# Group weights of the expert stage: one matmul per batch and row loads from DRAM in place of eight matmuls and eight evictions

## The chip, the cores and the metric

The kernel runs on one core of a Trainium2 chip. The metric is the device time of one execution in microseconds (us). Three runs of the kernel before gave a median of 1887.81 us (1886.92 to 1889.61).

## The reference

Two layers of gated attention and feed-forward are applied to `x`, 8 batches of 512 tokens by 512 features; each part adds `tanh(gate)` times its result to `x`. The change touches only the last part, the experts' layer:

```python
logits = jnp.einsum('th,eh->te', x, gate_weight)          # 32 experts
probs = jax.nn.softmax(logits)
top_val, top_idx = jax.lax.top_k(probs, 8)
top_val = top_val / jnp.sum(top_val, axis=-1, keepdims=True)
onehot = jax.nn.one_hot(merge_groups[top_idx], 8)
w_tg = jnp.einsum('tk,tkg->tg', top_val, onehot)          # weight of each of 8 groups
...                                                       # 8 groups of 192 hidden units
act = jax.nn.silu(gate) * up
y = jnp.einsum('tgi,ghi->tgh', act, dn)
out = jnp.einsum('tg,tgh->th', w_tg, y)
```

So each token has one weight for each of 8 groups, and that weight multiplies the 192 hidden units of the group before the down projection.

## The kernel before, in words

Everything is written out by hand from one list of steps, `make_plan()`. Each of the five engines walks through that same list in order and picks out the steps that concern it, so the list sets the order of work on every engine, on the queue of transfers (engine SP issues them all) and on PE. Semaphores join the engines.

The work has three stages: attention over 8 batches, the first feed-forward layer (until about 1063 us), and the expert stage with the second attention in between (from about 1063 us to the end). Weights and activations are kept as pairs of f16 tiles (high part, low part), so a projection of 128 output rows by 512 tokens takes 12 matmuls: three passes over four slices of 128.

**The expert stage** has 8 blocks, one for each batch b, of 12 steps j (8 groups of 192 rows are 1536 rows, 12 tiles of 128). One step, as (b, j), is:

- `ge` and `ue`: 12 matmuls each (line 923, in `project`), into one PSUM bank each. ScalarE (ACT) applies silu to the first (L1215), VectorE (DVE) multiplies the second by it (L1648), into one of three tiles `prod_s`.
- `mix`: DVE multiplies this tile by the group's weights (L1660) into `mact_s`; a tile that spans two groups (j = 1, 4, 7, 10) takes two instructions of 64 rows each. ACT rounds the result to f16 (L1228), GpSimd (POOL) makes the low part (L897).
- `dn` of the step before: 12 matmuls (L1092) that add into banks 0 to 3. `dn(b, j)` stands in the list behind `ge` and `ue` of step j+1, and waits for POOL's low part.

Before the first `mix` that uses group gg, the list has `bw(b, gg)`: PE multiplies `onehot` (a 0/1 matrix of 128 columns for each group, made once on DVE at L1410) by `wTs`, the turned weights of the 32 experts, so that all 128 output rows hold the weight of group gg (L1079); ACT evicts the bank into one of three tiles `gw_s` (L1223), and `mix` reads it. `bw(b, 0)` and `bw(b, 1)` come in steps 0 and 1, the others in steps 3, 4, 6, 7, 9 and 10.

Between these steps a list of side tasks of the next batch is taken one by one (`attention_tasks`): statistics (L1278, L852, L1283), norms (L1291) and turns on PE (L932, copied at L1131 and L1299), the attention over 64 context rows (`cxsplit`, L1522 and L1524, to `read`, L1587), the router, and `rturn` (L1063), which turns the experts' weights and leaves them in `wTs` (L1639). The two side tasks in step j = 1 and the one at the end of step 0 are: statistics of batch b+1 (step 0), then `cxsplit(b+1)` with `cxload(b+2)` and the first norm (step 1).

**The queue of engine SP** takes in block b, in the order of the list:

1. `xstore(E, b-1)`, 1 MB, L749, after the last `res3` of the block before (L1666, DVE, which follows the last `dn` of the batch);
2. `xload(E, b+2)`, 1 MB, L738, which waits until that store has landed;
3. `cxload(b+2)`, three transfers of 128 KB each, L809 to L811, which wait for `cxsplit(b+1)` on ACT and DVE in step 1.

The loads exist in blocks 1 to 5; blocks 6 and 7 have the store alone. Ahead of block 0 come the store of the stage before and `xload(E, 1)` and `xload(E, 2)` together (L738), which wait for that stage's last matmul; `cxload(2)` comes in its step 1.

```python
            elif kind == "mix":
                ...
                for gg in groups_of(j):
                    rows = slice(max(gg * INTER - j * P, 0), min((gg + 1) * INTER - j * P, P))
                    w.wait_ge(bw_ok, NG * b + gg + 1)
                    of = gw_s[(NG * b + gg) % 3]
                    e.tensor_tensor(r[rows, :], of[rows, :], m[rows, :], ALU.mult).then_inc(mixed)
```

Of the kernel before, what the change touches and what calls it, by code (L numbers as in the profile page):

```python
# [101 lines left out]
def make_plan():  # L102
# [260 lines left out]
    def attention_tasks(b):  # L363
        L, M = ln_tasks(("L", b)), ln_tasks(("M", b))

        def split():
            add("cxsplit", b)
            if b + 1 < NB:
                add("cxload", b + 1)

        def both(f, g):
            def go():
                f()
                g()
            return go
        return [L[0], both(split, L[1]), L[2], L[3], L[4], L[5], L[6],
                lambda: add("scores", b, banks=1), lambda: None, lambda: add("pturn", b, banks=1),
                lambda: add("read", b, banks=NT), *M, lambda: add("router", b, banks=1), lambda: None, lambda: None,
                lambda: add("rturn", b, banks=1)]

    for J in range(total + 2):
        if J < total:
# [31 lines left out]
    for J in range(total + 1):  # L414
        if J < total:
            b, j = divmod(J, NR)
            add("ge", b, j, banks=1)
            add("ue", b, j, banks=1)
            if side:
                side.pop(0)()  # L420
            for gg in range(j * P // INTER, ((j + 1) * P - 1) // INTER + 1):
                if gg * INTER >= j * P:
                    add("bw", b, gg, banks=1)
            add("mix", b, j)
        if J >= 1:
            bd, jd = divmod(J - 1, NR)
            add("dn", bd, jd)
            if jd == NR - 1:
                for t in range(NT):
                    add("res3", bd, t)  # L430
                if bd < NB - 1:
                    add("xstore", "E", bd)
                if bd + 3 < NB:
                    add("xload", "E", bd + 3)
        if J < total and j == 0 and b + 1 < NB:
            side = attention_tasks(b + 1)
        if side:
            side.pop(0)()
# [1 line left out]


def build(nc, x_in, ctx_in, ctx_t, mask_in, gx_in, gf_in, wq, wg, bg, wkv, wo, w1, b1, w2, b2,
          gw, gup, dnp, mg, dom, xa, xb, yscr, out, stack):
    plan = make_plan()
    nth, bank_of = plan.nth, plan.bank
    KB = 256
# [63 lines left out]
    prob = at(185, NT * NE).rearrange("p (t s) -> p t s", t=NT)  # L510
    prep = at(185.5, NT * NE).rearrange("p (t s) -> p t s", t=NT)
    wcat = small(NT * P // 2, F16).rearrange("p (t s) -> p t s", t=NT)
    onehot = small(NG * P // 2, F16)
    ctr = small(NC * CTX).rearrange("p (c s) -> p c s", c=NC)
    bgT, b1T = small(NC), small(NH)
    inv = {n: small(1) for n in ("q", "g", "1", "gate", "up", "gw")}
# [46 lines left out]
    def sem(name):  # L563
        return stack.enter_context(nc.semaphore(name))
# [27 lines left out]
    sc_mm, soft, sc_exp, p_turned, p_copied = (sem(n) for n in ("sc_mm", "soft", "sc_exp", "p_turned", "p_copied"))  # L592
    rd_mm, rd_c, rd_res = sem("rd_mm"), sem("rd_c"), sem("rd_res")
    r_mm, rout, r_exp, r_turned, r_copied = (sem(n) for n in ("r_mm", "rout", "r_exp", "r_turned", "r_copied"))
    ge_mm, silu, ue_mm, prod, bw_mm, bw_ok, mixed, m_hi, m_lo, dn_mm = (
        sem(n) for n in ("ge_mm", "silu", "ue_mm", "prod", "bw_mm", "bw_ok", "mixed", "m_hi", "m_lo", "dn_mm"))

    SOFT, ROUT = 13, 21
    C_MS, C_ID, C_ALL = 8, 9, 20
# [11 lines left out]
    def freed(step, i):  # L611
        kind, n = step[0], nth[step]
        if kind == "turn":
            return y_lo, n
        if kind == "q":
            return q_relu, n
        if kind == "gate":
            return g_tanh, n
        if kind == "kvk":
            return k_phi, n  # L620
        if kind == "kvv":
            return v_max, n
        if kind == "kvsum":
            return sum_ok, 4 * (n - 1) + i + 1
        if kind == "numden":
            return nd_mul, 2 * (n - 1) + i + 1
        if kind == "att":
            return a_gated, n
        if kind == "out":
            return res1, n  # L630
        if kind == "up":
            return gelu, n
        if kind == "scores":
            return soft, SOFT * (n - 1) + 4
        if kind == "pturn":
            return p_copied, n
        if kind == "read":
            return rd_res, NT * (n - 1) + i + 1
        if kind == "router":
            return rout, ROUT * (n - 1) + 1  # L640
        if kind == "rturn":
            return r_copied, n
        if kind == "ge":
            return silu, n
        if kind == "ue":
            return prod, n
        assert kind == "bw"
        return bw_ok, n


    x_slot = {("A", b): b % 3 for b in range(NB)}
# [58 lines left out]
    def bcast(v):  # L710
        return v.partition_broadcast(P)


    def sync_program(e):
        w = Once(e)
        regs = {}
        for step in plan.steps:
# [72 lines left out]
            elif kind == "small":  # L790
                e.dma_start(gains[:, 0:2], bcast(gx_in)).then_inc(small_in, 16)
                e.dma_start(gains[:, 2:4], bcast(gf_in)).then_inc(small_in, 16)
                e.dma_start(masku.bitcast(I32), bcast(mask_in.rearrange("b s -> (b s)"))).then_inc(small_in, 16)
                e.dma_start(bgT, bg.rearrange("(j p) -> p j", p=P), allow_slow_non_contiguous=True).then_inc(small_in, 16)
                e.dma_start(b1T, b1.rearrange("(j p) -> p j", p=P), allow_slow_non_contiguous=True).then_inc(small_in, 16)
                e.dma_start(mgi[0:NE, :], mg.rearrange("(e o) -> e o", o=1)).then_inc(small_in, 16)
                e.dma_start(mgi[NE:2 * NE, :], mg.rearrange("(e o) -> e o", o=1)).then_inc(small_in, 16)
                e.dma_start(domt[0:1, :], dom.rearrange("(o g) -> o g", o=1)).then_inc(small_in, 16)
            elif kind == "b2":
                w.wait_ge(a_turned, nth["att", NB - 1, NT - 1])  # L800
                e.dma_start(gb2, bcast(b2)).then_inc(b2_in, 16)
            elif kind == "cxload":
                b = step[1]
                if b == 0:
                    w.wait_ge(w_lo, nth["wlo", N_D - 1])
                else:
                    w.wait_ge(c_hi, 2 * b)
                    w.wait_ge(c_lo, 2 * b)
                e.dma_start(craw[0:CTX, :], ctx_in[b]).then_inc(craw_in, 16)  # L809
                e.dma_start(craw[CTX:P, :], ctx_in[b]).then_inc(craw_in, 16)  # L810
                e.dma_start(ctr, ctx_t[:, b * CTX:(b + 1) * CTX].rearrange("(c p) s -> p c s", p=P)).then_inc(craw_in, 16)  # L811
# [6 lines left out]
    def pool_program(e):  # L818
        w = Once(e)
        e.memset(ident, 0.0).then_inc(const)  # L820
        e.memset(bmask, 0.0).then_inc(const)
        e.memset(onehot, 0.0).then_inc(const)
        e.memset(wcat[:, :, :], 0.0).then_inc(const)
        e.memset(clo, 0.0).then_inc(const)
        e.memset(ones, 1.0).then_inc(const)
# [83 lines left out]
    def tensor_program(e):  # L909
# [25 lines left out]
        for step in plan.steps:  # L935
# [134 lines left out]
            elif kind == "ue":  # L1070
                _, b, j = step
                w.wait_ge(w_lo, n_lo["up"])
                project(step, upT, j, yT[b % 2], ue_mm)
            elif kind == "bw":
                _, b, gg = step
                k = bank_free(step)
                w.wait_ge(r_copied, b + 1)
                w.wait_ge(dconst, 13)
                e.matmul(bank[k][:, :], onehot[:, gg * P:(gg + 1) * P], wTs[b % 2], start=True, stop=True).then_inc(bw_mm)  # L1079
            elif kind == "dn":  # L1080
                _, b, j = step
                hv = macth_s[(n - 1) % 3]
# [40 lines left out]
    def scalar_program(e):  # L1123
        w = Once(e)
        for step in plan.steps:
# [81 lines left out]
            elif kind == "ge":  # L1207
# [5 lines left out]
                if n > 3:  # L1213
                    w.wait_ge(prod, n - 3)
                e.activation(silu_s[(n - 1) % 3], bank[bank_of[step, 0]][:, :], ACT.Silu,  # L1215
                             scale=inv["gate"]).then_inc(silu)
            elif kind == "bw":
                _, b, gg = step
                w.wait_ge(bw_mm, n)
                w.wait_ge(cd_ok, 1)  # L1220
                if n > 3:
                    w.wait_ge(mixed, mix_last(n - 3))
                e.activation(gw_s[(n - 1) % 3], bank[bank_of[step, 0]][:, :], ACT.Copy, scale=sc["kd"]).then_inc(bw_ok)  # L1223
            elif kind == "mix":
                w.wait_ge(mixed, mix_value(n))
                if n > 3:
                    w.wait_ge(dn_mm, dn_value(n - 3))
                e.activation(macth_s[(n - 1) % 3][0][:, 0, :], mact_s[(n - 1) % 3], ACT.Copy).then_inc(m_hi)  # L1228
# [18 lines left out]
    def vector_program(e):  # L1247
# [17 lines left out]
        for step in plan.steps:  # L1265
# [136 lines left out]
            elif kind == "tables":  # L1402
# [4 lines left out]
                w.wait_ge(dconst, 5)  # L1407
                w.wait_ge(const, C_ALL)
                for gg in range(NG):
                    e.tensor_scalar(onehot[0:2 * NE, gg * P:(gg + 1) * P], ones[0:2 * NE, :], mgf[0:2 * NE, :],  # L1410
                                    float(gg), ALU.mult, ALU.is_equal).then_inc(dconst)
            elif kind == "ctxmax":
                w.wait_ge(ctx_in_s, 16)
                e.tensor_reduce(sc["mc"], ctxT.rearrange("p t n -> p (t n)"), AX.X, ALU.max,
# [217 lines left out]
            elif kind == "rturn":  # L1632
# [2 lines left out]
                if b == 0:  # L1635
                    w.wait_ge(w_lo, nth["wlo", N_D - 1])
                if b > 1:
                    w.wait_ge(bw_mm, NG * (b - 1))
                e.tensor_copy(wTs[b % 2], bank[bank_of[step, 0]][:, :].bitcast(F16)[:, 0:TOK]).then_inc(r_copied)  # L1639
            elif kind == "ue":  # L1640
                _, b, j = step
# [8 lines left out]
            elif kind == "mix":  # L1650
# [4 lines left out]
                    w.wait_ge(m_lo, n - 3)  # L1655
                for gg in groups_of(j):
                    rows = slice(max(gg * INTER - j * P, 0), min((gg + 1) * INTER - j * P, P))
                    w.wait_ge(bw_ok, NG * b + gg + 1)
                    of = gw_s[(NG * b + gg) % 3]
                    e.tensor_tensor(r[rows, :], of[rows, :], m[rows, :], ALU.mult).then_inc(mixed)  # L1660
            elif kind == "res3":
                _, b, t = step
# [47 lines left out]
```

## Time and profile before

| what | value |
|---|---|
| median of 3 runs | 1887.81 us |
| the profiled execution's own time | 1887.19 us |
| its span in the trace | 1885.4 us |
| instructions | 24612 |
| moved by transfers | 112.10 MB, mean 59 GB/s |
| TensorE's mean granted clock | 0.993 of full speed |

The profiled execution is one run; its own time is 1.8 us more than the span of the trace, and 0.6 us less than the median of the three runs. Times in the trace count from the start of the span. A PE matmul of 512 columns is shown 379 ns long, but matmuls are pipelined: one starts some 0.216 us after another, so busy time adds up from starts, not from these lengths. "To landing" is the time from a transfer's issue until its semaphore is complete. The idle time in square brackets in a timeline is that of the engine just before the instruction, with the one that released it.

### The profile page before, as it was taken

The page shows a single profiled execution, that of the slowest core. Times are in us where ns is not written, and L with a number is a line of the kernel's source. Part 1 is how long each engine was busy: PE and PEld are TensorE (multiplying, and loading weights), DVE is VectorE, ACT ScalarE, POOL GpSimd, SP SyncE. Part 2 cuts the span into 40 slices and gives each one's busy share as a digit, 9 for nine tenths or more (in the row PEclk, how much of TensorE's full clock was granted, in tenths as well). Part 3 has the DMA queues.
Part 4 walks back from the last instruction along what each step waited for, and adds up shares of the span by engine and source line. Part 5 has one row for each costly group of instructions (what it writes and reads, how often), then busy time and mean ns, then how long its engine had stood idle before and what let it go on. Part 6 is the DMA issues. An engine that isn't in the chain of part 4 may idle for free.

```text
span 1885.4 us, 24612 instructions
## 1 busy us (share of the span) xinstructions
PE 1846.4 (98%) x9552; PEld 905.6 (48%) x9552; DVE 995.9 (53%) x2036; ACT 538.6 (29%) x801; POOL 323.5 (17%) x299
## 2 busy tenths in 40 slices
PE   8799999999999999999999999999999999999999
PEld 3445554644444444444444444444444444444444
DVE  5676776754554455454436554545445455554422
ACT  3224433312221122122112233233333223333321
POOL 1123322222021120202010011111111111111111
PEclk9899999999999999999999999999999999999999
DMA  5124433333414223340310200101010101000000
GB/s 159 55 62 129 140 118 95 96 129 65 104 42 127 90 68 104 70 125 27 90 54 9 76 1 23 32 1 54 1 54 1 54 1 54 1 23 1 1 23 23
DMA packets 135830, 112.10 MB, mean 59 GB/s; under 512 B 75554, under 2 KB 92066, under 8 KB 135714
## 3 DMA queue, kind: packets, MB, share of 16 engines
q1 hardware_dynamic: 135714, 110.53, 19.7%
q8 instruction: 75, 1.23, 0.3%
q14 instruction: 41, 0.34, 0.1%
HBM read 78.00 MB, written 32.51 MB: 59 GB/s over the span
## 4 chain that ended last, share of the span: by engine, by line
PE 83%; issue 9%; DVE 3%; POOL 2%; DMA 2%; ACT 1%; POOLq 0%; SPq 0%; DVEq 0%; ACTq 0%
PE bank L923 44%; PE bank L1012 17%; PE bank L1092 10%; PE bank L992 4%; PE bank L932 3%; PE bank L977 1%; POOL arena L897 1%; PE bank L958 1%; PE bank L1079 1%; PE bank L1027 1%; POOL arena L871 0%; PE bank L1054 0%; DVE arena L1278 0%; DMA arena<-in_L_xattn_Wkv 0%; DMA arena<-x_after_ffn 0%
## 5 line engine op out<-in xcount | busy, mean ns | idle before, releaser
L923 PE MATMUL bank<-arena 128*128 128x512 f16 x4608 | 1042.2, 380 | 8.4 <-DVE arena L1299 7.3
L923 PEld LDWEIGHTS bank<-arena 128*128 128x128 f16 x4608 | 451.1, 98 | 538.9 <-DVE arena L1299 7.8
L1012 PE MATMUL bank<-arena 128*128 128x512 f16 x1536 | 352.1, 379 | 1.2 <-DVE arena L1506 1.2
L1092 PE MATMUL bank<-arena 128*128 128x512 f16 x1152 | 264.3, 379 | 0.9 <-POOL arena L897 0.9
L1648 DVE SCALAR_TENSOR_TENSOR arena<-bank,arena 128x512 f32<-128x512 f32 x96 | 72.0, 750 | 329.0 <-PE bank L923 329.0
L1191 ACT ACTIVATE arena<-bank,arena 128x512 f32<-128x512 f32 x128 | 99.5, 778 | 493.5 <-PE bank L923 490.5
L1012 PEld LDWEIGHTS bank<-arena 128*128 128x128 f16 x1536 | 150.1, 98 | 181.1 <-DVE arena L1506 1.7
L897 POOL TENSOR_TENSOR arena<-arena 128x512 f16<-128x512 f32 x96 | 111.0, 1157 | 626.0 <-ACT arena L1228 626.0
L1504 DVE TENSOR_SCALAR arena<-arena 128x512 f16<-128x512 f32 x128 | 65.8, 514 | 281.6 <-ACT arena L1191 281.3
L1092 PEld LDWEIGHTS bank<-arena 128*128 128x128 f16 x1152 | 112.0, 98 | 128.4 <-POOL arena L897 1.4
L1506 DVE SCALAR_TENSOR_TENSOR arena<-arena 128x512 f16<-128x512 f32 x128 | 118.0, 922 | 4.6
L1215 ACT ACTIVATE arena<-bank,arena 128x512 f32<-128x512 f32 x96 | 66.0, 687 | 178.3 <-PE bank L923 178.2
L1228 ACT ACTIVATE arena<-arena 128x512 f16<-128x512 f32 x96 | 60.5, 630 | 197.0 <-DVE arena L1660 193.2
L1299 DVE TENSOR_TENSOR arena<-bank,arena 128x512 f16<-128x512 f32 x100 | 68.8, 689 | 70.9 <-ACT arena L1131 70.9
L1131 ACT ACTIVATE arena<-bank 128x512 f16<-128x512 f32 x100 | 59.3, 595 | 150.3 <-PE bank L932 149.9
L852 POOL TENSOR_TENSOR arena<-arena 128x4 f32<-128x4 f32 x32 | 38.0, 1186 | 347.0 <-DVE arena L1283 339.7
L1278 DVE BATCH_NORM_STATS2 arena<-arena 128x6 f32<-128x512 f32 x128 | 85.6, 669 | 21.3 <-DMA arena<-x_after_attention 15.2
L1660 DVE TENSOR_TENSOR arena<-arena 128x512 f32<-128x512 f32 (+1 forms) x128 | 87.8, 686 | 4.6 <-ACT arena L1223 3.1
L992 PE MATMUL bank<-arena 128*128 128x512 f16 x384 | 89.0, 383 | 0.0
L932 PE MATMUL bank<-arena 128*128 128x128 f32 x528 | 80.0, 277 | 7.8 <-DVE arena L1291 7.8
L1291 DVE TENSOR_SCALAR arena<-arena 128x512 f32<-128x512 f32 x128 | 74.0, 586 | 16.3 <-POOL arena L852 15.4
L932 PEld LDWEIGHTS bank<-arena 128*128 128x128 f32 x528 | 66.0, 143 | 30.0 <-DVE arena L1291 9.5
(159 smaller groups left out, 1215.8 us busy)
## 6 DMA issues: line engine op xcount, KB each, us to landing
arena<-in_L_ffn_proj SPq DMA_DIRECT2D x64, 256.0 KB, 2.9
arena<-in_L_ffn_gate_up_proj SPq DMA_DIRECT2D x96, 96.0 KB, 2.0
x_after_attention<-arena SPq DMA_DIRECT2D x8, 1024.0 KB, 5.2
arena<-x_after_attention SPq DMA_DIRECT2D x8, 1024.0 KB, 5.6
x_after_ffn<-arena SPq DMA_DIRECT2D x8, 1024.0 KB, 4.3
arena<-x_after_ffn SPq DMA_DIRECT2D x8, 1024.0 KB, 6.2
arena<-in_x SPq DMA_DIRECT2D x7, 1024.0 KB, 5.5
normalised_blocks<-arena SPq DMA_DIRECT2D x28, 256.0 KB, 2.0
```

What stands on the lines that cost most here:

```text
L897: e.tensor_tensor(rh[1][:, 0, :], r, rh[0][:, 0, :], ALU.subtract).then_inc(m_lo)
L923: m = e.matmul(bank[b][:, :], wT[l][:, c, tile * P:(tile + 1) * P], y[h][:, c, :], start=n == 0, stop=n == NPASS - 1)
L932: m = e.transpose(block4(b)[:, c, :], src[:, c * P:(c + 1) * P], ident)
L992: m = e.matmul(bank[k][:, :], aT[h][:, c, cols], woT[l][:, c, :], start=i == 0, stop=i == NPASS - 1)
L1012: m = e.matmul(bank[t][:, :], hv[h][:, 0, t * P:(t + 1) * P], w2T[l][:, j, :], start=j == 0 and i == 0, stop=j == NH - 1 and i == 2)
L1092: m = e.matmul(bank[t][:, :], hv[h][:, 0, t * P:(t + 1) * P], dnT[l][:, j, :], start=j == 0 and i == 0, stop=j == NR - 1 and i == 2)
L1191: e.activation(h_s[(n - 1) % 2], bank[bank_of[step, 0]][:, :], ACT.Gelu, bias=b1T[:, j:j + 1], scale=inv["1"]).then_inc(gelu)
L1278: e.bn_stats(stats[:, t, :], x[:, t, :]).then_inc(bn1)
L1291: e.tensor_scalar(yn_s[(n - 1) % 2], x[:, t, :], mv[:, t, 0:1], rs[:, t:t + 1], ALU.subtract, ALU.mult).then_inc(yn_ok)
L1506: e.scalar_tensor_tensor(out=hh[1][:, 0, :], in0=hs, scalar=sc["t1"], in1=hh[0][:, 0, :], op0=ALU.mult, op1=ALU.subtract).then_inc(h_lo)
L1648: e.scalar_tensor_tensor(out=m, in0=bank[bank_of[step, 0]][:, :], scalar=inv["up"], in1=silu_s[(n - 1) % 3], op0=ALU.mult, op1=ALU.mult).t ...
L1660: e.tensor_tensor(r[rows, :], of[rows, :], m[rows, :], ALU.mult).then_inc(mixed)
```

## The change

The step `bw` is gone. In its place, `gsum(b)` is a side task behind `rturn(b)`, in the last step of block b-1: one matmul with `of_group` (a 0/1 matrix whose column g marks the experts of group g) gives the weights of the 8 groups in rows 0 to 7 of a bank; ACT scales these 8 rows into `gsum_s`; SP stores them (16 KB) to `gscr` in DRAM. `gload(b, gg)` stands where `bw(b, gg)` stood: SP waits until the store has landed and until the tile of three has been read for the last time, and then loads the row of 512 weights into all 128 partitions of `gw_s` (256 KB). DVE's `mix` waits for this load. The diff, cut to its core:

```diff
                 lambda: add("read", b, banks=NT), *M, lambda: add("router", b, banks=1), lambda: None, lambda: None,
-                lambda: add("rturn", b, banks=1)]
+                lambda: add("rturn", b, banks=1), lambda: add("gsum", b, banks=1)]
...
             for gg in range(j * P // INTER, ((j + 1) * P - 1) // INTER + 1):
                 if gg * INTER >= j * P:
-                    add("bw", b, gg, banks=1)
+                    add("gload", b, gg)
             add("mix", b, j)
...
-    onehot = small(NG * P // 2, F16)
+    of_group = small(P // 2, F16)
+    gsum_s = small(TOK)
...
+            elif kind == "gsum":
+                b = step[1]
+                w.wait_ge(gs_ok, nth[step])
+                e.dma_start(gscr[b], gsum_s[0:NG, :]).then_inc(gs_out, 16)
+            elif kind == "gload":
+                _, b, gg = step
+                m = nth[step]
+                w.wait_ge(gs_out, 16 * (b + 1))
+                if m <= 3:
+                    w.wait_ge(down_mm, DN2 * NB)
+                else:
+                    w.wait_ge(mixed, mix_last(m - 3))
+                e.dma_start(gw_s[(m - 1) % 3], gscr[b, gg].partition_broadcast(P)).then_inc(gw_in[(m - 1) % 3], 16)
...
-            elif kind == "bw":
-                _, b, gg = step
+            elif kind == "gsum":
+                b = step[1]
                 k = bank_free(step)
-                w.wait_ge(r_copied, b + 1)
+                w.wait_ge(r_copied, n)
                 w.wait_ge(dconst, 13)
-                e.matmul(bank[k][:, :], onehot[:, gg * P:(gg + 1) * P], wTs[b % 2], start=True, stop=True).then_inc(bw_mm)
+                e.matmul(bank[k][:, :], of_group, wTs[b % 2], start=True, stop=True).then_inc(gs_mm)
...
-            elif kind == "bw":
-                _, b, gg = step
-                w.wait_ge(bw_mm, n)
+            elif kind == "gsum":
+                w.wait_ge(gs_mm, n)
                 w.wait_ge(cd_ok, 1)
-                if n > 3:
-                    w.wait_ge(mixed, mix_last(n - 3))
-                e.activation(gw_s[(n - 1) % 3], bank[bank_of[step, 0]][:, :], ACT.Copy, scale=sc["kd"]).then_inc(bw_ok)
+                if n > 1:
+                    w.wait_ge(gs_out, 16 * (n - 1))
+                e.activation(gsum_s[0:NG, :], bank[bank_of[step, 0]][0:NG, :], ACT.Copy,
+                             scale=sc["kd"][0:NG, :]).then_inc(gs_ok)
...
                 for gg in range(NG):
-                    e.tensor_scalar(onehot[0:2 * NE, gg * P:(gg + 1) * P], ones[0:2 * NE, :], mgf[0:2 * NE, :],
-                                    float(gg), ALU.mult, ALU.is_equal).then_inc(dconst)
+                    e.tensor_scalar(of_group[0:2 * NE, gg:gg + 1], mgf[0:2 * NE, :], float(gg), None,
+                                    ALU.is_equal).then_inc(dconst)
...
                 for gg in groups_of(j):
                     rows = slice(max(gg * INTER - j * P, 0), min((gg + 1) * INTER - j * P, P))
-                    w.wait_ge(bw_ok, NG * b + gg + 1)
-                    of = gw_s[(NG * b + gg) % 3]
+                    of, k = gw_s[(NG * b + gg) % 3], NG * b + gg
+                    w.wait_ge(gw_in[k % 3], 16 * (k // 3 + 1))
                     e.tensor_tensor(r[rows, :], of[rows, :], m[rows, :], ALU.mult).then_inc(mixed)
```

`mix_last(n)` is the count of `mixed` after the last instruction that reads the n-th group's weights.

## Rows read from the trace of the kernel before

**Rows 1.** The page, whole span: busy us, share, instructions by engine.
```profile
PE 1846.4 (98%) x9552; PEld 905.6 (48%) x9552; DVE 995.9 (53%) x2036; ACT 538.6 (29%) x801; POOL 323.5 (17%) x299
```

**Rows 2.** The waits of engine PE: us in total, times, longest.
```profile
PE bank L1012 <- DVE arena L1506: 1.2, 1, 1.2
...
PE bank L1092 <- POOL arena L897: 0.9, 1, 0.9
```

**Rows 3.** Line L1079: count, ns (min/median/max), first and last start.
```profile
L1079 PE MATMUL bank<-arena x64: 379/379/380, 1068.2 to 1867.6; 128*128 128x512 f16 x64
```

**Rows 4.** Timeline at block 3: start, us, engine, line, operation [idle before].
```profile
1376.55 0.69 DVE L1660 TENSOR_TENSOR arena<-arena 128x512 f32<-128x512 f32 x1 [0.29 <-ACT arena L1223]
...
1379.91 0.38 SPq L749 DMA_DIRECT2D out<-arena  x1
...
1383.30 0.38 PE L1079 MATMUL bank<-arena 128*128 128x512 f16 x1
...
1385.68 1.40 DVE L1660 TENSOR_TENSOR arena<-arena 64x512 f32<-64x512 f32 x2
...
1386.11 5.34 PE L923 MATMUL bank<-arena 128*128 128x512 f16 x24
1386.53 0.59 SPq L811 DMA_DIRECT2D arena<-in_ctx_turned  x1
...
1387.82 1.16 POOL L897 TENSOR_TENSOR arena<-arena 128x512 f16<-128x512 f32 x1 [3.45 <-ACT arena L1228]
...
1391.72 2.75 PE L1092 MATMUL bank<-arena 128*128 128x512 f16 x12
```

**Rows 5.** Landing times of the loads of L811 in blocks 1 to 5.
```profile
DMA to landing us min/median/max: 4.6/4.7/6.0
```

**Rows 6.** The same timeline where block 1 begins.
```profile
1180.72 0.59 SPq L811 DMA_DIRECT2D arena<-in_ctx_turned  x1
...
1185.26 2.75 PE L1092 MATMUL bank<-arena 128*128 128x512 f16 x12
```

**Rows 7.** Timeline of SP: a store, then the bias row spread.
```profile
389.65 0.36 SPq L749 DMA_DIRECT2D x_after_attention<-arena  x1
390.05 0.50 SPq L801 DMA_DIRECT2D arena<-in_L_ffn_proj_bias  x1
```

**Rows 8.** Landing time of that store (L749).
```profile
DMA to landing us min/median/max: 4.8/4.8/4.8
```

**Rows 9.** Landing time of that bias row (L801).
```profile
DMA to landing us min/median/max: 5.1/5.1/5.1
```

**Rows 10.** The view of DMA issues: count, KB each, median us to landing.
```profile
arena<-in_L_ffn_proj SPq DMA_DIRECT2D x64, 256.0 KB, 2.9
...
normalised_blocks<-arena SPq DMA_DIRECT2D x28, 256.0 KB, 2.0
```

**Rows 11.** Timeline where block 0 begins.
```profile
1064.46 1.67 SPq L738 DMA_DIRECT2D arena<-x_after_ffn  x2
...
1072.29 0.69 DVE L1278 BATCH_NORM_STATS2 arena<-arena 128x6 f32<-128x512 f32 x1 [2.18 <-DMA arena<-x_after_ffn]
...
1073.82 2.75 PE L1092 MATMUL bank<-arena 128*128 128x512 f16 x12
...
1078.72 0.59 SPq L811 DMA_DIRECT2D arena<-in_ctx_turned  x1
...
1082.03 2.75 PE L1092 MATMUL bank<-arena 128*128 128x512 f16 x12
```

**Rows 12.** Landing times of the two loads of L738 ahead of block 0.
```profile
DMA to landing us min/median/max: 7.8/8.9/9.9
```

**Rows 13.** Timeline of engine PE, after a wait of 5.51 us.
```profile
71.57 3.41 PE L968 MATMUL bank<-arena 128*128 128x132 f32 x16 [5.51 <-DVE arena L1433]
```

**Rows 14.** Stretches: us, busy PE, PEld, DVE, ACT, POOL, clock, DMA, GB/s.
```profile
71.57:74.98 3.41, 3.41 (x16) 3.21 (x16) 0.87 (x3) 0.00 (x0) 0.10 (x1) 0.59 0.02 5
397.81:401.22 3.41, 3.41 (x16) 1.57 (x17) 3.37 (x3) 0.78 (x1) 3.41 (x3) 1.00 0.00 0
```

More of the change, by code:

```diff
@@ L442, in build @@
 def build(nc, x_in, ctx_in, ctx_t, mask_in, gx_in, gf_in, wq, wg, bg, wkv, wo, w1, b1, w2, b2,
-          gw, gup, dnp, mg, dom, xa, xb, yscr, out, stack):
+          gw, gup, dnp, mg, dom, xa, xb, yscr, gscr, out, stack):
     plan = make_plan()
@@ L594, in build @@
     r_mm, rout, r_exp, r_turned, r_copied = (sem(n) for n in ("r_mm", "rout", "r_exp", "r_turned", "r_copied"))
-    ge_mm, silu, ue_mm, prod, bw_mm, bw_ok, mixed, m_hi, m_lo, dn_mm = (
-        sem(n) for n in ("ge_mm", "silu", "ue_mm", "prod", "bw_mm", "bw_ok", "mixed", "m_hi", "m_lo", "dn_mm"))
+    ge_mm, silu, ue_mm, prod, gs_mm, gs_ok, mixed, m_hi, m_lo, dn_mm = (
+        sem(n) for n in ("ge_mm", "silu", "ue_mm", "prod", "gs_mm", "gs_ok", "mixed", "m_hi", "m_lo", "dn_mm"))
+    gs_out, gw_in = sem("gs_out"), [sem(f"gw_in{i}") for i in range(3)]
     SOFT, ROUT = 13, 21
@@ L646, in freed @@
             return prod, n
-        assert kind == "bw"
-        return bw_ok, n
+        assert kind == "gsum"
+        return gs_ok, n
     x_slot = {("A", b): b % 3 for b in range(NB)}
@@ L821, in pool_program @@
         e.memset(bmask, 0.0).then_inc(const)
-        e.memset(onehot, 0.0).then_inc(const)
+        e.memset(of_group, 0.0).then_inc(const)
         e.memset(wcat[:, :, :], 0.0).then_inc(const)
@@ L1637, in vector_program @@
                 if b > 1:
-                    w.wait_ge(bw_mm, NG * (b - 1))
+                    w.wait_ge(gs_mm, b - 1)
                 e.tensor_copy(wTs[b % 2], bank[bank_of[step, 0]][:, :].bitcast(F16)[:, 0:TOK]).then_inc(r_copied)
@@ L1704 @@
     yscr = nc.dram_tensor("normalised_blocks", (2, TOK, D), F32, kind="Internal").ap()
+    gscr = nc.dram_tensor("group_weights", (NB, NG, TOK), F32, kind="Internal").ap()
     out = nc.dram_tensor("out", (NB, TOK, D), F32, kind="ExternalOutput").ap()
     with ExitStack() as stack:
-        build(nc, *args, xa, xb, yscr, out, stack)
+        build(nc, *args, xa, xb, yscr, gscr, out, stack)
     r = run_bass_kernel_spmd(nc, [arrays], core_ids=[0])
```

## The prediction

> **What bounds the kernel.** I read the page first, then PE's waits, then the timeline where one batch ends and the next begins, then the landing times of the transfers there. The page shows PE busy for 98% of the span [rows 1]. Nearly all that PE waits is before the expert stage; in the stage, the waits view has one wait, 0.9 us for POOL at the very end [rows 2]. So a matmul taken out of this stage shortens the run by its pitch, and any wait put in front of PE lengthens it. The other engines have room on the whole, but the low part of a `mix` comes just in time at one place, and the timeline shows how much room is left there.
>
> **What is removed.** PE has 64 `bw` matmuls [rows 3] and keeps 8 `gsum` matmuls of the same size, so 56 go. From the `bw` at 1383.30 to the next projection at 1386.11 are 13 matmuls in 2.81 us, 0.216 us each [rows 4]: 56 x 0.216 = **-12.1 us**, all of it on the path. ACT loses 56 evictions; it was not late anywhere, so I count nothing. The smaller one-hot preparation on DVE, and its smaller memset, I count at nothing too: the work lies in the early stage, is done once, and can give back 1 us at most.
>
> **What is added, one by one.**
>
> *gsum on PE.* It stands ahead of `ge` and `ue` of step 0. Back from the `bw` at 1383.30 there are two pairs of projections, one `dn` and one `bw`, 61 matmuls or 13.2 us: it starts at 1370.1. The copy that it waits for reads the four turns ahead of the `dn` before it, so it has that `dn`'s 2.6 us (12 x 0.216). No wait.
>
> *The first load of a block.* `gsum` at 1370.1, ACT some 1 us later, so the store goes out at 1371.3. A store takes 2.0 us at 256 KB [rows 10]; 16 KB can't be far below. The load goes out at 1373.3 and, at 2.9 us for a 256 KB load [rows 10], lands at 1376.2. `mix(b, 0)` starts at 1376.55 [rows 4], and can start 0.3 us earlier without the eviction that released it. So it is just hidden: I take 0. The bounds are 0 and 2.1 us (with 5.1 us of [rows 9] for the load). Were it late, `res3`, the store and all behind them would be late by as much.
>
> *The second load of a block* is what decides. It is needed by the second half of `mix(b, 1)`, but on SP it stands behind the store, the 1 MB load and the three context loads, the last of which is issued at 1386.53 and takes 0.59 us [rows 4]. So `gload(b, 1)` is issued at 1387.1, when the half-`mix` that reads it has already begun: that pair runs from 1385.68 to 1387.08 [rows 4]. And it stands on the same queue as a load of 1 MB that has just begun. The last context load lands 4.7 us after issue (median of five, [rows 5]), at 1391.2. What do 256 KB more cost behind a big transfer? [rows 7] show the same form, one row of 2 KB spread over 128 partitions, issued 0.4 us behind a 1 MB store: the store lands at 389.65 + 4.8 = 394.45 [rows 8], the row at 390.05 + 5.1 = 395.15 [rows 9], 0.7 us later. So the weights land at 1391.9. From there the chain is half a `mix` (0.69), ACT and POOL: from 1386.4, where the second half began, to POOL's end at 1388.98 are 2.6 us, and PE needs 0.1 more: `dn(b, 1)` can start at 1394.6. Before it started at 1391.72 [rows 4], and one `bw` less lies ahead of it: 1391.5. **Stall 3.1 us** in each of blocks 2 to 5, 12.4 us. In block 1 the context load lands 6.0 us after 1180.72 [rows 5, 6], so 1186.7 + 0.7 + 2.7 = 1190.1 against 1185.26 - 0.2: **5.0 us**. In blocks 6 and 7 only the 1 MB store is ahead. In block 3 it went out at 1379.91 [rows 4]; a row issued 0.4 us behind it lands 5.1 us later, at 1385.4, and the half-`mix` that reads it began at 1386.4 (without the context's work before it, some 1 us sooner). Nothing is charged.
>
> *Block 0.* `gload(0, 0)` stands behind the two 1 MB loads [rows 11], the second of which lands 9.9 us after its issue at 1065.0 [rows 12], at 1074.9; with 0.7 us, 1075.6. A whole `mix`, ACT and POOL take 2.7: 1078.3. `dn(0, 0)` was at 1073.82, less two `bw`, 1073.4: **4.9 us**. Behind the late `mix` DVE has the statistics, which began at 1072.29 and now begin at 1076.3. From their start to the end of issuing the context loads were 7.0 us (1072.29 to 1078.72 + 0.59), so `gload(0, 1)` goes out at 1083.3, lands at 1086.2 (2.9 us) and allows `dn(0, 1)` at 1088.9; it is due 8.21 us after the first `dn` (1073.82 to 1082.03), at 1086.5: **2.4 us**.
>
> *The other loads.* Groups 2 to 7 are issued when a tile of three has been read for the last time, one to two steps of 8 us before use; 2.9 us are hidden. After a stall DVE and ACT catch up while PE runs the late `dn` and the next two projections, so a stall happens once a block.
>
> *The clock.* A stall can cost twice. After a wait of 5.51 us [rows 13] PE's clock was at 0.59 of full on average over its next 3.41 us [rows 14], that is mostly at 1.2 GHz in place of 2.4: 3.41 x 0.41 = 1.4 us lost; I take 1.5 with the edges. After the wait of 1.2 us [rows 2], in dense work, it stayed at 1.00 [rows 14]. My seven stalls lie between, from 2.4 to 5.0 us, so from 0 to 7 x 1.5 = 10.5 us. I charge five of them, the shorter ones being nearer to the harmless row: **+7.5 us**. The Trainium skill (TensorE: Matmul & The Clock Gate, Part 1: The HAM clock gate) calls the half rate the idle default which activity lifts, and puts the ramp's penalty at under 1% of a typical span; what follows a wait in the rows agrees, but here the ramp would be paid up to seven times.
>
> **Sum** against the profiled execution's own 1887.2: -12.1 + 12.4 + 5.0 + 4.9 + 2.4 + 7.5 = +20.1, 1907.3 us. The median of the runs shown is 0.6 above that execution: **1908 us**. With no fall of the clock it is 1900.4, with seven 1911.
>
> **Rivals.** *Faster: the loads overtake.* If a group load didn't wait for the transfers ahead of it on the queue, it would land by its own latency. With 2.9 us: 1387.1 + 2.9 + 2.7 = 1392.7, a stall of 1.2 in blocks 2 to 5, 1.8 in block 1; in block 0 none at the first `dn` and 1079.3 + 5.6 - 1081.5 = 3.4 at the second: 10 us given back, some 1886, no change. With 2.0 us, the shortest of [rows 10], 0.3 x 4 + 0.9 + 2.5 = 4.6 given back: **1880.3 us**. It decides from where the stalls add up to under 12 us, about 1.7 us each. Against it: context loads of 128 KB take 4.7 us here, and the row of [rows 9] came in behind its store. The Trainium skill (DMA: Bandwidth & Descriptors, Queues, rings and completion order) says completion "is not FIFO per issuing engine", which is this rival, though it has each engine take its descriptors in order; by it alone the sum would be 1880 to 1886. Chance 0.14: 0.08 for the faster half, 0.06 for no change.
>
> *Slower still: the spread read is slow, or the round trip through DRAM late.* If 5.1 us were the row's own time, 3.1 above the 2.0, it would land 2.4 us later than I have it behind the loads (7 stalls, +16.8), and the first load of each block 2.1 us late, which pushes the store and the 1 MB load (5 blocks, +10.5), and all seven falls are paid (+3): 1938 us. The 0.7 us of [rows 7 to 9] speaks against it. Chance 0.10.
>
> *The change doesn't do what it says*: the matmuls could go and nothing else be seen, if `mix` had slack for all of this: 1887.8 - 12.1 = 1875.7. It would need the row at 1388.8, 1.7 us after issue with a megabyte ahead. Chance 0.04.
>
> **Numbers.** The forecast keeps 0.72. The range takes the clock at either end (1900 to 1911), 1 us per stall in the landing either way (7), and part of the slow rival: **1892 to 1928**. About 0.2% (3.8 us) is what a measurement can tell from no change. Faster 0.12, same 0.07, slower 0.81.
>
> **What would show it.** In the profile of the changed kernel: L1079's successor with 8 matmuls; new PE waits for POOL in front of `dn`, seven of over 2 us, at the starts of blocks 0 to 5 only, and behind them DVE waiting for a transfer at `mix`; the load of the second group issued right behind L811's successor and landing near 5 us, other group loads near 2.9; PE's clock at half speed behind some stalls. I am wrong if PE waits less than 12 us in the stage, or if it waits inside blocks too.

## The result and the profile after

| | before | changed |
|---|---|---|
| median of the runs beside each other | 1888.24 us | 1913.10 us (1907.95 to 1916.08) |
| the profiled execution: own time, span | 1887.19, 1885.4 | 1907.95, 1906.2 |
| mean granted clock of PE, profiled execution | 0.993 | 0.991 |

The ratio of the times is 1.0128, with a 95% interval of 1.0116 to 1.0141: 24.9 us slower at the medians. The profiled execution is the fastest of the four runs of the changed kernel; the others have a mean clock of 0.983 to 0.985, which will matter below.

The page of the changed kernel, its first part, the down projection of the expert stage in its fifth (busy us, mean ns, idle before), and the DMA issues:

```profile
PE 1838.9 (96%) x9496; PEld 897.1 (47%) x9496; DVE 993.7 (52%) x2036; ACT 499.7 (26%) x745; POOL 321.9 (17%) x299
...
L1108 PE MATMUL bank<-arena 128*128 128x512 f16 x1152 | 271.1, 386 | 25.8 <-POOL arena L913 25.8
...
L1676 DVE TENSOR_TENSOR arena<-arena 128x512 f32<-128x512 f32 (+1 forms) x128 | 87.6, 684 | 45.4 <-DMA arena<-group_weights 43.7
...
arena<-group_weights SPq DMA_DIRECT2D x64, 256.0 KB, 3.2
```

56 matmuls are gone (9496 against 9552), PE is busy 7.5 us less than in [rows 1], and yet the span grew by 20.8. The waits view of PE has the place; it answers to [rows 2], where the same line had one wait of 0.9 us:

```profile
PE bank L1108 <- POOL arena L913: 25.8, 9, 5.1
```

Nine waits, 25.8 us. From the timeline, in blocks 0 to 5: 4.8 and 1.4 us (block 0), then 5.1, 3.5, 3.8, 2.9 and 3.5 us, one each at the start of blocks 1 to 5; one of 0.2 us later in block 3, and the 0.9 us at the end that was there before. None at the start of blocks 6 and 7. Here is the start of block 3 again, in the changed kernel; it answers to [rows 4] (the `bw` at 1383.30 has no successor there):

```profile
1392.68 0.69 DVE L1676 TENSOR_TENSOR arena<-arena 128x512 f32<-128x512 f32 x1
...
1396.04 0.39 SPq L752 DMA_DIRECT2D out<-arena  x1
...
1400.34 0.37 SPq L741 DMA_DIRECT2D arena<-x_after_ffn  x1
...
1401.84 0.68 DVE L1676 TENSOR_TENSOR arena<-arena 64x512 f32<-64x512 f32 x1
...
1402.69 0.59 SPq L827 DMA_DIRECT2D arena<-in_ctx_turned  x1
1403.33 1.45 SPq L817 DMA_DIRECT2D arena<-group_weights  x3
...
1408.96 0.69 DVE L1676 TENSOR_TENSOR arena<-arena 64x512 f32<-64x512 f32 x1 [6.44 <-DMA arena<-group_weights]
...
1409.68 0.63 ACT L1244 ACTIVATE arena<-arena 128x512 f16<-128x512 f32 x1 [10.91 <-DVE arena L1676]
...
1410.38 1.15 POOL L913 TENSOR_TENSOR arena<-arena 128x512 f16<-128x512 f32 x1 [9.89 <-ACT arena L1244]
...
1411.59 0.61 PE L1108 MATMUL bank<-arena 128*128 128x512 f16 x2 [3.76 <-POOL arena L913]
```

The reader sees the chain whole. The first half of `mix(3, 1)` runs at 1401.84; the second waits 6.44 us for `group_weights`. That row's load is issued at 1403.33, right behind the last context load, 7.29 us after the store at 1396.04, and the half-`mix` begins 5.6 us after that. Then ACT and POOL, and PE stands still for 3.76 us. `mix(3, 0)`, at 1392.68, waits for nothing.

### The profile page after: what moved, and what is told of

Same layout as the page of the kernel before. It is cut to its first block, busy times and chain, and to the rows that moved or that the text cites. A ratio compares the mean times of both kernels' runs of the same rounds, so it can differ in the third digit from the quotient of the medians.

```text
span 1906.2 us, 24523 instructions
## 1 busy us (share of the span) xinstructions
PE 1838.9 (96%) x9496; PEld 897.1 (47%) x9496; DVE 993.7 (52%) x2036; ACT 499.7 (26%) x745; POOL 321.9 (17%) x299
## 4 chain that ended last, share of the span: by engine, by line
PE 77%; issue 11%; DVE 4%; DMA 3%; POOL 3%; ACT 1%; SPq 0%; POOLq 0%; DVEq 0%; ACTq 0%
PE bank L939 39%; PE bank L1028 17%; PE bank L1108 10%; PE bank L1008 4%; PE bank L948 2%; POOL arena L913 2%; PE bank L993 1%; PE bank L974 1%; DMA arena<-group_weights 1%; DVE arena L1294 1%; DMA arena<-in_x 1%; DMA x_after_attention<-arena 1%; POOL arena L868 1%; POOL arena L887 0%; PE bank L1043 0%
## 5 line engine op out<-in xcount | busy, mean ns | idle before, releaser
L1108 PE MATMUL bank<-arena 128*128 128x512 f16 x1152 | 271.1, 386 | 25.8 <-POOL arena L913 25.8
```

The costliest lines, as they stand in the source:

```text
L1108: m = e.matmul(bank[t][:, :], hv[h][:, 0, t * P:(t + 1) * P], dnT[l][:, j, :], start=j == 0 and i == 0, stop=j == NR - 1 and i == 2)
```

## The experiments

The theory: only the second group's load in blocks 1 to 5, and the first two loads in block 0, are late; they are late by their place on SP's queue, partly because they are issued late and partly because of the bytes around them; and each wait costs again through PE's clock. Rivals: the spread load is slow in itself or its traffic hurts others; the waits are due to the way through DRAM; only the time of issue counts; the clock costs nothing. "Waits" below are PE's waits for POOL in the stage, in the profiled execution. The kernel before beside these runs was at 1887.4 to 1888.1 us.

| run | what differs from the changed kernel | median us | waits us | ratio to before (95%) |
|---|---|---|---|---|
| e0_again | nothing | 1913.5 | 26.8 | 1.0133 (1.0117 to 1.0148) |
| e1_blocks | blocks 1 to 7: second load right behind the first | 1883.4 | 6.8 | 0.9977 (0.9967 to 0.9987) |
| e2_block0 | block 0: both loads ahead of the 2 MB | 1903.6 | 20.5 | 1.0086 (1.0068 to 1.0104) |
| e3_both | both | 1875.4 | 2.2 | 0.9933 (0.9917 to 0.9950) |
| e4_traffic | `mix` waits for no load; `bw` back | 1890.7 | 0.9 | 1.0014 (1.0005 to 1.0024) |
| e5_before_ctx | second load ahead of the context loads | 1898.9 | 17.8 | 1.0055 (1.0041 to 1.0069) |
| e6_big_behind | the megabyte 0.55 us behind it | 1909.9 | 22.3 | 1.0113 (1.0098 to 1.0129) |
| e7_pad | 12 matmuls ahead of each late `dn` | 1904.4 | 13.5 | 1.0086 (1.0072 to 1.0099) |
| e8_big_away | the megabyte 1.0 us behind it | 1898.7 | 19.4 | 1.0059 (1.0042 to 1.0075) |
| e9_ctx_away | the contexts 1.1 us behind it | 1894.5 | 15.8 | 1.0032 (1.0020 to 1.0045) |
| e10_big_gone | the megabyte some 8 us behind it | 1898.4 | 17.7 | 1.0059 (1.0042 to 1.0075) |
| e11_ctx_gone | the contexts far behind it | 1894.6 | 15.5 | 1.0031 (1.0017 to 1.0046) |

**The changed kernel again** (e0_again).

> The changed kernel again, unchanged, as the measure for the runs beside it. 1913 us, between 1908 and 1916.

1913.5 us: as said.

**Is it the place on the queue?** e1_blocks, e2_block0 and e3_both move loads in the list and nothing else:

in the loop over the steps of the stage (e1_blocks, e3_both)

```diff
-            for gg in range(j * P // INTER, ((j + 1) * P - 1) // INTER + 1):
-                if gg * INTER >= j * P:
+            for gg in range(NG):
+                due = (gg * INTER) // P
+                if gg == 1 and b > 0:
+                    due = 0
+                if due == j and ("gload", b, gg) not in P_.nth:
                     add("gload", b, gg)
```

and ahead of the stage (e2_block0, e3_both)

```diff
+    add("gload", 0, 0)
+    add("gload", 0, 1)
     add("xload", "E", 1)
     add("xload", "E", 2)
```

> The changed kernel, with the load of the second group of blocks 1 to 7 moved on SP's queue to right behind the first group's load, ahead of the store, the 1 MB load and the context loads. Theory (that load is late because of its place on SP): the waits of PE for POOL at the start of blocks 1 to 5 (5.1, 3.5, 3.8, 2.9, 3.5 us, 18.7 in all) go, with the clock's falls behind them; block 0 keeps its two (4.8 and 1.4 us): 1888.2 - 12.1 + 6.1 + some 2 for the clock = 1884 us. Rival (the spread load is slow in itself, or the added traffic slows PE and DVE): the waits stay near what they are, 1905 us or more. Rival (PE gains less than 12.1 us from 56 matmuls): 1890 us or more with the waits gone.

Measured 1883.4 us, where 1884 was expected; the five waits are gone, block 0's two stay (4.85 and 0.90).

> The changed kernel, with the loads of groups 0 and 1 of block 0 moved on SP's queue ahead of the two 1 MB loads before that block; blocks 1 to 7 as in the changed kernel. Theory: the two waits of block 0 (4.8 and 1.4 us) and the fall of the clock behind the first (1.7 us) go, those of blocks 1 to 5 stay: 1913.1 - 6.1 - 1.7 = 1905 us. Rival (the late first load is due to the store and load through DRAM): block 0's waits stay, 1913 us.

Measured 1903.6 us, where 1905 was expected. Block 0's two waits of 4.8 and 1.4 us became one of 0.8; those of blocks 1 to 5 stay (5.1, 3.0, 4.0, 3.3, 3.3).

> Both moves together. Theory: no wait of PE in the expert stage but the 0.9 us at the end, 1888.2 - 12.1 = 1876 us, faster than the kernel before. Rival (traffic or something else takes part of the gain): 1880 to 1890 us.

Measured 1875.4 us, 12.3 below the kernel before, which is what 56 matmuls of 0.216 us take (12.1). PE's waits in e3_both, the line of the stage:

```profile
PE bank L1113 <- POOL arena L918: 2.2, 3, 1.2
```

The expectation had no wait but the 0.9 us at the end. There are two more, 1.2 us in block 0 (`mix(0, 1)` waits for no transfer there, it comes behind other work on DVE) and 0.2 in block 3. Even so the way through DRAM is no obstacle (the round trip is still there for every block), and order on one queue accounts for the whole loss, as far as the times can tell: by the interval of the ratio the gain is 9.4 to 15.7 us. e3_both is faster than both kernels.

**Does the traffic cost anything?** e4_traffic keeps `gsum`, its store and all 64 loads at their places, but lets them land in three tiles that nothing reads (each load now also waits until the one before it in its tile has landed); `mix` reads the evicted banks of the old eight matmuls:

```diff
+                    add("bw", b, gg, banks=1)
                     add("gload", b, gg)
...
-                e.dma_start(gw_s[(m - 1) % 3], gscr[b, gg].partition_broadcast(P)).then_inc(gw_in[(m - 1) % 3], 16)
+                e.dma_start(gdum[(m - 1) % 3], gscr[b, gg].partition_broadcast(P)).then_inc(gw_in[(m - 1) % 3], 16)
...
-                    w.wait_ge(gw_in[k % 3], 16 * (k // 3 + 1))
+                    w.wait_ge(bw_ok, k + 1)
```

> The changed kernel with the eight matmuls and evictions per batch brought back, and mix reading their result as in the kernel before; the one matmul, the store to DRAM and the 64 spread loads stay as they are, but land in tiles that nothing reads. Theory (only the wait for the data costs, not the traffic or SP's longer list): 1888.2 + 8 x 0.216 = 1890 us, no wait of PE in the stage. Rival (16.8 MB more of traffic, or the stores and loads of x held up on SP, cost time of their own): 1895 us or more.

Measured 1890.7 us against 1887.6 beside it: 3.1 us for 8 matmuls more, 1.7 of which are their pitch. The one wait in the stage is the old one:

```profile
PE bank L1123 <- POOL arena L922: 0.9, 1, 0.9
```

That leaves 1.4 us for 16.8 MB more of traffic and the longer list; with the interval of the ratio (0.9 to 4.5 us above the kernel before) it is 2.8 us at most. The waits for data are the cost.

**Does the clock cost?** e7_pad puts 12 matmuls, whose bank nothing reads, right ahead of `dn(b, 1)` in blocks 1 to 5:

```diff
             bd, jd = divmod(J - 1, NR)
+            if jd == 1 and 0 < bd < 6:
+                add("pad", bd, banks=1)
             add("dn", bd, jd)
...
+                for i in range(12):
+                    m = e.matmul(bank[k][:, :], upT[0][:, 0, 0:P], yT[b % 2][0][:, 0, :], start=i == 0, stop=i == 11)
```

> The changed kernel with 12 matmuls (2.6 us) added on PE right before the late down projection of blocks 1 to 5, into a bank that nothing reads. The waits there shrink from 18.7 us to about 5.7, and 13 us of work are added, so the stalls themselves cost the same. Theory (the waits also cost by the clock's falls behind them): PE's clock no longer falls in blocks 2 to 5 and the time goes down to about 1907 us. Rival (the clock costs nothing): 1913 us as before.

Measured 1904.4 against 1913.5 beside it: **9.1 us faster with 13.0 us of useless work added**. PE's waits in e7_pad, the line of the stage:

```profile
PE bank L1119 <- POOL arena L918: 13.5, 9, 4.7
```

The waits shrank by 13.3 us, from 26.8 to 13.5, so work and waits cancel to 0.3 us, and 8.8 us are left for the clock. The traces bear this out: in e0_again six of the seven `dn` behind a long wait are longer than 2.76 us, by 13.3 us in all; in e7_pad one is, that of block 0, by 2.3. These 11.0 us are nearly the whole difference of the two profiled executions (11.9 us). The mean granted clock went from 0.986 to 0.993. The windows view shows one fall. In e0_again, the `dn` behind the wait of block 3 (stretch, busy us of PE, PEld, DVE, ACT, POOL, granted clock, DMA share, GB/s):

```profile
1412.68:1417.98 5.30, 5.30 (x13) 2.07 (x14) 1.78 (x4) 0.63 (x1) 1.15 (x1) 0.50 0.15 49
```

and the same `dn` in the profiled execution of the changed kernel, behind an even longer wait:

```profile
1411.59:1414.35 2.76, 2.76 (x14) 1.38 (x15) 1.79 (x4) 0.63 (x1) 0.23 (x1) 1.00 0.00 0
```

5.30 us at 1.2 GHz in place of 2.76 at 2.4: 2.5 us lost behind a wait of 3.39 us, nothing behind one of 3.76. So the length of the wait alone doesn't decide.

**What makes the load late: issue, or the bytes around it?** Six runs move one thing each: the load itself, the megabyte, or the three context loads. "Landing" is that of the second group's load after its own issue, mean of blocks 1 to 5.

e5_before_ctx, ahead of the side task that holds `cxload`:

```diff
+            if j == 1 and b > 0:
+                add("gload", b, 1)
```

e6_big_behind, behind `gload(b, 1)`, with the old place of `xload` removed:

```diff
+            if j == 1 and b > 0 and b + 2 < NB:
+                add("xload", "E", b + 2)
```

e8_big_away and e10_big_gone are the same with `j == 3` and `j == 6`, behind `mix`; e9_ctx_away and e11_ctx_gone leave `xload` and put `add("cxload", b + 2)` there with `j == 3` and `j == 6`.

> The changed kernel with the second group's load of blocks 1 to 7 moved ahead of the three context loads only; the store and the 1 MB load stay ahead of it. It is then issued some 2.5 us sooner in blocks 2 to 5. Theory (it lands 0.7 us behind whatever is ahead of it on the queue): it lands 0.7 us after the 1 MB load, 1.2 us sooner than now, and PE's waits in blocks 1 to 5 shrink from 18.7 to about 13 us: 1905 us. Rival (only the time of issue counts): it lands 2.5 us sooner, waits of 6 us, 1897 us. Rival (the context loads are what hold it up, not the megabyte): waits near 0, 1889 us.

Measured 1898.9 us, waits of blocks 1 to 5 of 11.0 us. Issued 4.7 us after the store in blocks 2 to 5, landing 6.3 us later. In block 3 the 1 MB load landed 5.5 us after its issue at 1398.22, at 1403.7, and the row at 1404.7, 1.0 us behind it. The mechanism held (it lands right behind the megabyte, not 2.5 us sooner), but I had its gain too small: it landed some 1.7 us sooner than in the changed kernel, not 1.2. The time is nearer to the 1897 of the rival, whose landing, 2.5 us sooner, didn't come.

> The changed kernel with the 1 MB load of x moved behind the second group's load; that load's place behind the store and the context loads, and so its time of issue, stays. Theory (part of the lateness is issue, part is the megabyte ahead on the rings): it lands 3.1 us after issue instead of 5.7, the waits of blocks 1 to 5 shrink by 2.6 each to about 6 us, 1897 us. Rival (the order on the rings doesn't matter): waits as now, 1913 us.

Measured 1909.9 us, waits of 16.5 in blocks 1 to 5. **The expectation fell.** Landing was 5.1 us, not 3.1. SP's timeline in block 3, and the landing time of the first row load in it:

```profile
1402.02 0.59 SPq L827 DMA_DIRECT2D arena<-in_ctx_turned  x1
1402.65 0.50 SPq L817 DMA_DIRECT2D arena<-group_weights  x1
1403.20 0.43 SPq L741 DMA_DIRECT2D arena<-x_after_ffn  x1
```

```profile
DMA to landing us min/median/max: 4.7/4.7/4.7
```

Either the contexts ahead hold it up, or the megabyte issued 0.55 us later does.

> The changed kernel with the 1 MB load of x moved two steps on (behind the mix of step 3), so that the second group's load of blocks 1 to 5 has only the three context loads ahead and no megabyte ahead of it or right behind it. In the run with the megabyte right behind it, that load landed 4.7 us after its issue, not the 3.1 I expected. Theory A (a transfer issued 0.5 us later on the same queue shares the engines with it): it now lands 3.7 to 4.2 us after issue, as the load of block 0 does that has only the context loads ahead; PE's waits in blocks 1 to 5 fall from 16.5 to about 11 us, 1902 us. Theory B (the context loads ahead, half of them in runs of 256 bytes, are what holds it up): it lands 4.7 us after issue as before, 1910 us.

Measured 1898.7 us, but the landing (4.5, 5.6, 3.5, 4.5, 4.3 us, mean 4.5) fits neither number: between step 1 and step 3 of the list SP has nothing to wait for, so the megabyte went out 1.0 us behind the row, not two steps later. (Of the three context loads one has runs of 256 bytes, not half of them.)

> The changed kernel with the three context loads moved two steps on (behind the mix of step 3), so that the second group's load is issued right behind the 1 MB load of x, with no context loads ahead or behind. Theory A (what is issued right behind a load shares the engines with it): it lands sooner than in the run with the contexts right behind it (6.1 us after issue there), near 5.2, waits of blocks 1 to 5 about 7 us, and block 0's second wait goes too, about 1892 us. Theory B (only what is ahead counts): it lands 6.1 us after issue, waits of 11 us, 1897 us.

Measured 1894.5 us, waits of 9.9 in blocks 1 to 5, landing 6.1: nearer to theory B, with the same flaw, the contexts went out 1.1 us behind. Block 0's second wait is gone, but it is gone in e6_big_behind too, which changes nothing in block 0. Two more runs put the transfer behind a load that SP really has to wait with:

> As the run with the megabyte moved two steps on, but placed behind the load of the fifth group (step 6), which waits for DVE, so that the megabyte really goes out some 8 us later and not 1 us as there. The second group's load then has the contexts ahead, another row load right behind it, and nothing else. Theory A (what is issued right behind shares the engines): it lands 3.7 to 4.2 us after issue in blocks 1 to 5, waits there sum to 6 to 10 us, 1896 us. Theory B (only what is ahead counts): it lands near 4.7 to 5.1 us after issue, waits of 15 us, 1903 us or more.

Measured 1898.4 us, landing 4.0, 4.4, 3.3, 4.3, 4.4 us, mean 4.1, waits of 11.2: the landing of theory A, with waits a little above its 6 to 10. SP's timeline of block 3:

```profile
1396.88 0.59 SPq L827 DMA_DIRECT2D arena<-in_ctx_turned  x1
1397.52 8.09 SPq L817 DMA_DIRECT2D arena<-group_weights  x4
1405.65 0.43 SPq L741 DMA_DIRECT2D arena<-x_after_ffn  x1
```

> The same with the three context loads in place of the megabyte: they really go out some 8 us later, the megabyte stays right ahead of the second group's load. Theory A: what followed it 1 us behind slowed it, so it now lands near 5.5 us after issue in place of 6.4, waits of blocks 1 to 5 fall by 0.9 each to about 5 us. Theory B: it lands 6.4 us after issue as before, waits of 9 to 10 us, 1894 us.

Measured 1894.6 us, landing 6.0, waits of 9.7. The waits and the time are those of theory B, and the landing is within 0.1 us of the 6.1 of e9_ctx_away.

Taken together: a row load lands 3.0 to 3.2 us after issue when little is near it (minimum and median of the 64). With the contexts ahead it is 4.1 (e10; another row load is issued 0.5 us behind it there, and the two shares weren't separated). A megabyte **behind** it, by 0.55 us, adds 1.0 more (e6: 5.1). A megabyte 0.4 us **ahead** makes it 6.0 (e11), contexts behind that 0.1 to 0.2 more (e9, e5), which is within the scatter of five landings. The megabyte ahead shows on the contexts too: with no megabyte ahead, the last of them lands 2.5 to 2.6 us after its issue (e10, all five blocks), in the changed kernel 4.7 to 5.9. So theory A is right for the megabyte and B, within what five landings can tell, for the contexts. The Trainium skill (DMA: Bandwidth & Descriptors, Queues, rings and completion order) says that each engine takes its descriptors in ring order while a later one may finish its write before an earlier one; e5 agrees with the first half. No run here shows the second: in block 3 of e6 the megabyte issued later lands at 1410.1, behind the row at 1407.4. What e6 against e10 shows is that it costs the earlier transfer 1.0 us. Which engine of the 16 came last, and why, was not looked at.

The need follows from the timeline: `dn(b, 1)` isn't late if the row lands 8.9 us after the store's issue (1391.5 - 2.7 - 1379.9, from [rows 4]). The changed kernel issues it at 7.3 and lands it at 12.7; e6 12.4, e10 11.4, e5 11.0, e11 10.7. None of them reaches 8.9, and the waits of some 3.7, 3.3, 2.2, 2.2 and 1.9 us a block are these differences, to within 0.3 us. Issued at 7.3, even a row load all alone (3.2) would be late by 1.6 us. Of the moves tried, only the one ahead of the store does it. A place between the store and the 1 MB load was not tried; blocks 6 and 7 of the changed kernel, where the row goes out 0.43 us behind the store and lands 5.2 to 5.3 us later, 5.7 after the store's issue, without a wait of PE, suggest that it would do too.

## Why the prediction was right

The time was 1908 forecast and 1913.1 measured, inside the range, and slower as forecast. The mechanism is the one forecast: late loads at the starts of blocks 0 to 5, by their place on the queue, and the clock behind the waits. The waits were forecast at 24.7 us and are 24.9 in the profiled execution; part of that is luck, as the terms for block 0 and for blocks 1 to 5 are off by 1.2 and 1.3 us in opposite directions. Step by step:

- **The gain, -12.1 us.** e3_both is 12.3 us below the kernel beside it (9.4 to 15.7).
- **gsum and the first load of a block, 0.** Right, and with more margin than I gave it: the store goes out 1.1 us after `gsum` begins (1386.30, 1387.42), the load 1.46 us behind the store, not 2.0, lands 3.0 us later, at 1391.9, and `mix` starts at 1392.68 without a wait.
- **The second load, 5.0 + 4 x 3.1 = 17.4 us.** 18.7 in the profiled execution (5.1, 3.5, 3.8, 2.9, 3.5). The issue was as worked out (7.29 us after the store, from the kernel before 7.2). The landing in block 3 came at 12.9 us from the store, where I had 12.0. The 0.7 us from the context load's landing to the row's held: it is 0.6 to 0.7 in all five blocks. The term that was short is the landing of the last context load, for which I took 4.7 us. In blocks 1 to 5 of the changed kernel (L827):

```profile
DMA to landing us min/median/max: 4.7/5.3/5.9
```

In block 3 it is 5.6, in the kernel before 4.6. A row load now follows 0.64 us behind it; whether that is the cause was not tested.

- **Block 0, 4.9 + 2.4.** 4.8 and 1.4. The load landed at 1066.42 + 9.4 = 1075.8, where I had 1075.6. The second wait came out shorter, and the first `dn` ran partly at half clock (4.45 us in place of 2.76), which makes the second due 1.7 us later: a fall of the clock pays for part of the next wait.
- **Blocks 6 and 7, nothing.** Right; the row landed 5.2 to 5.3 us after issue behind the store, where [rows 9] had 5.1, and PE didn't wait.
- **The clock, 5 falls x 1.5 = 7.5 us.** This is the mis-sized term. In the profiled execution 4 of the 7 `dn` behind a long wait are longer, by 6.6 us in all, close to 7.5. But that is the fastest of four executions (1907.95 us, mean clock 0.991; the others 0.983 to 0.985). In the profiled execution of e0_again (1916.1 us, the slowest of its four, mean clock 0.986) it is 6 of 7 and 13.3 us, 2.2 us a fall. The waits of the two differ by 1.0 us, the falls by 6.7. So most of the 5 us between my number and the median is likely this term, though the median's execution has no trace. The price was short because I took 1.4 us from [rows 14], a stretch at 0.59; a whole `dn` at 0.50 costs 2.5. The trace of the kernel before had this dearer case as well, 12 matmuls behind a wait of 4.30 us:

```profile
297.45 5.30 PE L923 MATMUL bank<-arena 128*128 128x512 f16 x12 [4.30 <-DVE arena L1299]
```

The four runs span 8.1 us, against 2.7 for the kernel before beside them; the four of e0_again span 3.2.

- **The rivals.** "The loads overtake" fell in both halves: the row lands behind the megabyte. "The spread read is slow" fell: 3.2 us alone. "Not what it says" fell: PE waits 25.8 us in the stage.
- **The signs.** I had said seven waits of over 2 us, and that a wait inside a block would show me wrong. Six are over 2 us, and one of 0.15 us is inside block 3. It is there in e1_blocks and e3_both as well, so it doesn't come from the loads that they move.

Summed for the profiled execution from e3_both's span: 1873.7 + (25.8 - 2.2) + 6.6 = 1903.9, of 1906.2. For e0_again it is 1873.7 + (26.8 - 2.2) + 13.3 = 1911.6, of 1914.4. Of the 2.3 and 2.8 us left, 1.2 lie ahead of the stage, whose last store goes out at 1064.28 and 1064.26, in e3_both at 1063.07. A fall can also outlast the `dn`: the four turns behind it in block 3 take 0.83 us in e0_again and 0.60 in the changed kernel. The rest was not traced.

## What to carry to other kernels

A transfer that replaces a computation needs a place on its queue as well as a price: read what stands ahead of it in that queue's own order, with the waits of each, and compare the landing with the moment when the chain behind it becomes late. Put a small load with a near deadline ahead of the large ones that have a far one; here a move of a few lines in the list turned 25 us lost into 12 us gained. And when PE must stand still for some microseconds anyway, count the clock behind the wait too: filling the gap with useless matmuls was 9 us faster than leaving it empty.

## What the runs showed of the hardware that was not expected

- PE's clock behind a wait. In the profiled executions of the changed kernel and of the twelve runs above, PE waits 93 times for POOL in this stage. Behind all 13 waits of 4.7 us and more the following `dn` was lengthened by a fall to 1.2 GHz; behind none of the 48 under 1.96 us; of the 32 between, behind 22, with no clear order by length (3.76 us was followed by a fall in one run and not in another). Two executions of the same kernel lost 6.6 and 13.3 us in this way. In windows of 1 us the granted clock is below 1.00 in four stretches of the stage in the first and in six in the second, each at one of the long waits; in the kernel before, in e3_both and in e4_traffic, where no wait of the stage is over 1.2 us, it is 1.00 for as long as PE works.
- A 1 MB load issued 0.55 us behind a 256 KB load on the same queue delayed the earlier one by 1.0 us (5.1 against 4.1, means of five).
- The eviction of 8 rows by 512 on ACT took as long as that of 128 rows, 0.68 us (L1223 in the kernel before, median of 64: 0.687):

```profile
1386.71 0.68 ACT L1238 ACTIVATE arena<-bank,arena 8x512 f32<-8x512 f32 x1 [0.69 <-PE bank L1095]
```
